# Weight conversion of the first pass: 228 interleaved items through SBUF in place of HBM-to-HBM casts and phase-wise items

## Chip, cores and metric

The kernel runs on all 8 cores of one Trainium2 chip. Each core works on its own 4096 of the 32768 tokens and on a full copy of all weights; the cores exchange nothing. The metric is the device time in microseconds of the slowest core, from one launch.

## What is computed

```python
x = x + attn(layernorm(x))          # x: [4, 8192, 2048] f32
x = x + ffn(layernorm(x))

def attn(x):                        # identity = x
    xn = (x - mu) * rsqrt(var + 1e-5) * gamma + beta
    z, gate = split(xn @ W_in.T, 2)             # W_in [8192, 2048] f32
    z = z * sigmoid(clip(z, -15, 15)) * softmax(-dt)
    return (z * silu(clip(gate, -15, 15))) @ W_out.T + x   # W_out [2048, 4096] f32

def ffn(x):                         # weights are int32 in 0..255
    deq = lambda wq, s: (wq - 128.0) * s[:, None]
    h = silu(x @ deq(wq_gate, s_gate).T) * (x @ deq(wq_up, s_up).T)   # 5632 wide
    return h @ deq(wq_down, s_down).T
```

## The kernel before

A core takes its 4096 tokens in 8 passes of 512 (NP = 8). In each pass the weights stream once from HBM in slabs of 128 x 2048 bf16, 512 KB each, 304 slabs per pass, through a ring of 7 buffers wb (NWB). SyncE issues all slab loads in the order of their use (gen_sync), each after the matmuls of the slab seven places earlier are done. A pass has these stages on PE (gen_tensor): transposes of the normalized tokens (xn4, then xnT); the in projection, 32 gate iterations e of two slabs (z and gate) with 16 matmuls each; the out projection in two halves P2 of 32 slabs for 256 tokens each; transposes again; the gate and up projections, 44 iterations h of two slabs (wg, wu); the down projection in two halves of 44 slabs (wd).

VectorE works in program order (gen_vector2): first the softmax of dt and the statistics of the first LayerNorm (ln1_block); then for each e the clipping and products of the gate (label gat:p:e); for each P2 the residual and the statistics of the second LayerNorm (st2:p:P2); for each h the product actb (actf:p:h); at the end the final sums. PE may be two iterations ahead of VectorE in both loops, since it waits for gat of e-2 and actf of h-2.

The matmuls read bf16 copies of the weights in HBM, called win_s, wout_s, wg_s, wu_s and wd_s. They are made once, during the first pass (p = 0), and every core makes them for itself. There are two ways. The float32 weights win (64 slabs) and wout (32) are cast by DMAs from HBM to HBM that GpSimd issues at the start: 16 of 4 slabs and 4 of 8 slabs. The int32 weights go through SBUF, one item per slab, 132 items. For each item GpSimd issues a load (qld) of 1024 KB into one of two buffers qi; VectorE converts it into one of two buffers qo (wq_op: subtract 128, for wd also times the scale sdbt); GpSimd stores qo to HBM and issues the load of the item two further on:

```python
            for i_ in range(3 * NH):
                u.wait(E, f"wqts:{i_}")            # conversion i_ done
                ii = E.dma_start(wq_dst(i_), qo[i_ % 2][:, :]) if E else None
                u.inc(f"qo{i_ % 2}", 16, f"wqst:{i_}", ii)
                if i_ + 2 < 3 * NH:
                    qld(i_ + 2)
```

The items come in the order all wg, all wu, all wd. VectorE's program places them: two after each gate iteration e, 12 after each P2, two after each of the first 22 iterations h. SyncE's slab loads of the first pass wait for the cast of their chunk (semaphores wc, oc), or for gdone, udone and ddone, which GpSimd raises when all 44 items of a kind have landed.

Of the kernel before, what the change touches and what calls it, by code (L numbers as in the profile page):

```python
# [63 lines left out]
def build_program():  # L64
# [27 lines left out]
    with contextlib.ExitStack() as st:  # L92
        def sb(name, shape, dt):
# [30 lines left out]
                     + [f"qo{i}" for i in range(2)]  # L124
                     + [f"x{i}" for i in range(8)]
                     + [f"wc{i}" for i in range(16)]
                     + [f"oc{i}" for i in range(4)])
# [55 lines left out]
        def gen_gpsimd(E):  # L183
# [15 lines left out]
            for c in range(16):  # L199
                i = None  # L200
                if E:
                    src = winT[4 * c:4 * c + 4].rearrange("E p c -> (E p) c")
                    dst = win_s[4 * c:4 * c + 4].rearrange("E p c -> (E p) c")
                    i = E.dma_start(dst, src, max_dma_last_dim=8192)
                u.inc(f"wc{c}", 16, f"cast:win:{c}", i)
                if c == 3:
                    u.wait(E, "dtwrow")
                    dma("dt2", dtw_s[:, :], dt_row, label="dtwst")
                    u.wait(E, "dtwst")
                    in_ap = dtw_s[:, :].rearrange("a (j p) -> p (a j)", p=128) if E else None  # L210
                    i2 = E.dma_start(dtwt[:, 0:NZ], in_ap, allow_slow_non_contiguous=True) if E else None
                    u.inc("dt3", 16, "dtwcols", i2)
            for c in range(4):
                i = None
                if E:
                    src = woutT[1024 * c:1024 * (c + 1), :]
                    dst = wout_s[1024 * c:1024 * (c + 1), :]
                    i = E.dma_start(dst, src, max_dma_last_dim=8192)
                u.inc(f"oc{c}", 16, f"cast:wout:{c}", i)

            def wq_src(i_):
                if i_ < NH:
                    return wqg[i_]
                if i_ < 2 * NH:
                    return wqu[i_ - NH]
                k = i_ - 2 * NH
                return wqd[k * 128:(k + 1) * 128, :]

            def wq_dst(i_):
                if i_ < NH:  # L230
                    return wg_s[i_]
                if i_ < 2 * NH:
                    return wu_s[i_ - NH]
                k = i_ - 2 * NH
                return wd_s[k * 128:(k + 1) * 128, :]

            def qld(i_):
                ii = E.dma_start(qi[i_ % 2][:, :], wq_src(i_)) if E else None
                u.inc(f"qi{i_ % 2}", 16, f"qld:{i_}", ii)
# [3 lines left out]
            for i_ in range(3 * NH):  # L243
                u.wait(E, f"wqts:{i_}")
                ii = E.dma_start(wq_dst(i_), qo[i_ % 2][:, :]) if E else None
                u.inc(f"qo{i_ % 2}", 16, f"wqst:{i_}", ii)
                if i_ + 2 < 3 * NH:
                    qld(i_ + 2)
                if i_ in (NH - 1, 2 * NH - 1, 3 * NH - 1):
                    u.wait(E, f"wqst:{i_ - 1}")  # L250
                    u.wait(E, f"wqst:{i_}")
                    if E:
                        E.sem_inc(sems["g"], 1)
                    u.inc("g", 1, {NH - 1: "gdone", 2 * NH - 1: "udone", 3 * NH - 1: "ddone"}[i_], None)
            u.wait(E, f"wqts:{3 * NH - 2}")
            dma("x6", xslot(1, 2), x_in[T + 256:T + 384, :], label="xin:1:2")
            u.wait(E, f"wqts:{3 * NH - 1}")
# [172 lines left out]
        def gen_vector2(E):  # L430
# [6 lines left out]
            def wq_op(i_):  # L437
# [3 lines left out]
                if i_ < 2 * NH:  # L441
# [270 lines left out]
```

How the kernel before makes its waits and increments, by code:

```python
    def inc(self, sem, n, label=None, instr=None):  # L47
# [5 lines left out]
                assert self.lab[label] == (sem, self.cnt[sem]), (label, self.lab[label], sem, self.cnt[sem])  # L53
        if instr is not None:
            instr.then_inc(self.sems[sem], n)
# [1 line left out]
    def wait(self, E, label):  # L57
        if E is None:
            return
        sem, val = self.lab[label]
        E.wait_ge(self.sems[sem], val)
# [121 lines left out]
        def gen_gpsimd(E):  # L183
# [80 lines left out]
                        u.wait(E, f"fin:{p}:{tc}" if j == 3 else f"finj:{p}:{tc}:{j}")  # L264
                        ii = E.dma_start(out_hbm[r0:r0 + 128, j * T:(j + 1) * T],
                                         gsc[2 * j + 1][:, :]) if E else None
                        u.inc(f"od{j}", 16, f"oD:{p}:{tc}:{j}", ii)
                    if p + 2 < NP:
                        r1 = (p + 2) * T + tc * 128
                        ii = E.dma_start(xslot(p + 2, tc), x_in[r1:r1 + 128, :]) if E else None
                        u.inc(f"x{4 * (p % 2) + tc}", 16, f"xin:{p + 2}:{tc}", ii)
            if E:
                for jj in range(4):
                    E.wait_ge(sems[f"od{jj}"], u.cnt[f"od{jj}"])
# [156 lines left out]
            def op(fn, label=None):  # L431
                if E:
                    E.wait_ge(sems["v"], u.cnt["v"])
                i = fn() if E else None
                u.inc("v", 1, label, i)
# [123 lines left out]
            def op(fn, label=None):  # L559
                if E:
                    E.wait_ge(sems["s"], u.cnt["s"])
                i = fn() if E else None
                u.inc("s", 1, label, i)
```

## Time and profile before

| | us |
|---|---|
| timed runs, lowest and highest of 2 | 8082.6 and 8993.11 |
| their median | 8537.86 |
| profiled execution | 8093.98 |
| its span, slowest core | 8092.3 |
| spans of the 8 cores | 8056.6 to 8092.3 |
| mean granted PE clock | 0.903 to 0.907 |
| PE busy | 6723.5 (83%) |
| VectorE busy | 1992.1 (25%) |
| ScalarE busy | 923.4 (11%) |

All cores do the same work on other tokens, and end within 0.5% of each other. The profile shows the slowest core, and splits its span: the granted clock is a share of full speed (1.0 is 2.4 GHz), the DMA share is the mean busy share of the core's 16 DMA engines. POOL is GpSimd, DVE is VectorE, ACT is ScalarE, SPq is SyncE's DMA queue; busy microseconds stand per engine, and an idle time in square brackets names what ended it.

### The profile page before, as it was taken

How to read it: one execution, taken by the hardware profiler on the slowest of the kernel's cores; microseconds unless marked ns; L12 is line 12 of the kernel's file. 1: busy time of each engine (PE TensorE's matmuls, PEld its weight loads, DVE VectorE, ACT ScalarE, POOL GpSimd, SP SyncE). 2: the span in 40 equal slices, each digit the busy share in tenths (PEclk: the TensorE clock that was granted, in tenths of full speed). 3: DMA queues.
4: the chain of work that ended last, by engine and by line, in shares of the span. 5: the costliest groups of instructions: out<-in, count | busy, mean ns of one | idle time of the engine just before them, and what ended most of it. 6: DMA issues, size and time to landing. Idle time of an engine off the chain costs nothing.

```text
span 8092.3 us, 83398 instructions; the slowest of 8 cores (8056.6 to 8092.3 us)
## 1 busy us (share of the span) xinstructions
PE 6723.5 (83%) x30208; PEld 2977.7 (37%) x30208; DVE 1992.1 (25%) x3488; ACT 923.4 (11%) x1330; POOL 246.1 (3%) x458
## 2 busy tenths in 40 slices
PE   1026646799889998999799998999799989999898
PEld 0002212344334443444344443444344434444343
DVE  1014333214311232114211331114211431123210
ACT  1000010002111111011100111011110211111100
POOL 1001111000000000000000000000000000000000
PEclk8568878899999998999899998999899999999898
DMA  9999979785636754484546654584547563665447
GB/s 149 109 179 306 304 254 306 254 258 175 213 125 197 237 186 150 154 283 151 184 152 224 212 195 143 169 267 160 178 152 265 171 208 130 202 213 184 154 152 238
DMA packets 416528, 1606.83 MB, mean 199 GB/s; under 512 B 46224, under 2 KB 46320, under 8 KB 395008
## 3 DMA queue, kind: packets, MB, share of 16 engines
q1 hardware_dynamic: 350208, 1275.22, 48.5%
q0 software_dynamic: 65920, 326.28, 16.0%
q8 instruction: 250, 4.10, 0.2%
q14 instruction: 150, 1.23, 0.1%
HBM read 1548.87 MB, written 153.11 MB: 210 GB/s over the span
## 4 chain that ended last, share of the span: by engine, by line
PE 74%; DMA 10%; DVE 6%; another core or an unknown queue 6%; issue 2%; ACT 2%; POOL 1%; DVEq 0%; ACTq 0%; POOLq 0%; SPq 0%
PE pb L315 74%; DMA qi<-wqg 3%; DMA qi<-wqd 3%; DMA qi<-wqu 3%; ACT xnT L578 1%; DVE gsc L508 1%; DVE bnb L456 1%; DMA out<-gsc 1%; DVE qo L442 1%; DVE qo L444 1%; DVE xres L511 1%; DVE gsc L553 0%; ACT xn L602 0%; ACT xnT L607 0%
## 5 line engine op out<-in xcount | busy, mean ns | idle before, releaser
L315 PE MATMUL pb<-xnT,wb 128*128 128x512 bf16 x19456 | 4341.7, 387 | 714.8 <-DVE actb L497 542.1
L315 PEld LDWEIGHTS pb<-xnT,wb 128*128 128x128 bf16 x19456 | 1930.5, 99 | 3122.4 <-issue 918.7
L315 PE MATMUL pb<-wb,actb 128*128 128x512 bf16 x9728 | 2215.6, 390 | 253.4 <-DVE gsc L553 70.7
L315 PEld LDWEIGHTS pb<-wb,actb 128*128 128x128 bf16 x9728 | 967.1, 100 | 1500.4 <-issue 449.3
L535 DVE SCALAR_TENSOR_TENSOR actb<-pb,suct,gsc 128x512 bf16<-128x512 f32 x352 | 264.2, 751 | 2165.2 <-PE pb L315 2162.7
L616 ACT ACTIVATE gsc<-pb,sgct 128x512 f32<-128x512 f32 x352 | 242.4, 689 | 2322.4 <-PE pb L315 2322.3
L315 PE MATMUL pb<-idmt,xn 128*128 128x128 bf16 x1024 | 167.5, 291 | 382.5 <-ACT xn L602 165.4
L588 ACT ACTIVATE gsc<-gsc 128x512 f32<-128x512 f32 x256 | 161.5, 631 | 1941.1 <-DVE gsc L492 1941.0
L492 DVE TENSOR_SCALAR gsc<-pb 128x512 f32<-128x512 f32 x256 | 177.0, 691 | 618.7 <-PE pb L315 558.5
L442 DVE TENSOR_SCALAR qo<-qi 128x2048 bf16<-128x2048 int32 x88 | 108.0, 1227 | 697.3 <-DMA qi<-wqg 518.5
L265 POOL DMA_DIRECT2D out<-gsc x128 | 69.0, 540 | 6463.0 <-DVE gsc L553 6442.7
L315 PEld LDWEIGHTS pb<-idmt,xn 128*128 128x128 bf16 x1024 | 80.1, 115 | 473.1 <-issue 472.1
L495 DVE TENSOR_TENSOR gsc<-gsc 128x512 f32<-128x512 f32 x256 | 177.1, 692 | 255.1 <-ACT gsc L590 255.1
L578 ACT ACTIVATE xnT<-pb,bcct,gcct 128x512 bf16<-128x512 f32 x128 | 99.8, 780 | 913.6 <-PE pb L315 901.9
L497 DVE SCALAR_TENSOR_TENSOR actb<-gsc,dtwt 128x512 bf16<-128x512 f32 x256 | 192.2, 751 | 26.9 <-DVE gsc L496 0.5
L493 DVE TENSOR_SCALAR gsc<-pb 128x512 f32<-128x512 f32 x256 | 176.8, 690 | 28.5 <-DVE gsc L492 1.9
L496 DVE TENSOR_TENSOR gsc<-pb,gsc 128x512 f32<-128x512 f32 x256 | 177.1, 692 | 26.6
L553 DVE TENSOR_TENSOR gsc<-xres,pb 128x512 f32<-128x512 f32 x64 | 44.0, 687 | 539.1 <-PE pb L315 492.0
L590 ACT ACTIVATE gsc<-gsc 128x512 f32<-128x512 f32 x256 | 161.5, 631 | 43.4 <-DVE gsc L493 42.3
L444 DVE SCALAR_TENSOR_TENSOR qo<-qi,sdbt 128x2048 bf16<-128x2048 int32 x44 | 100.8, 2292 | 175.5 <-DMA qi<-wqd 175.3
L508 DVE TENSOR_SCALAR gsc<-xres,coef 128x512 f32<-128x512 f32 x64 | 35.0, 546 | 364.9 <-PE pb L315 358.4
L553 DVE TENSOR_TENSOR gsc<-qi,pb 128x512 f32<-128x512 f32 x32 | 22.0, 687 | 342.8 <-PE pb L315 322.9
(77 smaller groups left out, 955.0 us busy)
## 6 DMA issues: line engine op xcount, KB each, us to landing
wb<-wd_s SPq DMA_DIRECT2D x704, 512.0 KB, 5.2
wb<-win_s SPq DMA_DIRECT2D x512, 512.0 KB, 3.3
wb<-wout_s SPq DMA_DIRECT2D x512, 512.0 KB, 4.8
wb<-wg_s SPq DMA_DIRECT2D x352, 512.0 KB, 3.3
wb<-wu_s SPq DMA_DIRECT2D x352, 512.0 KB, 3.3
qi<-wqg POOLq DMA_DIRECT2D x44, 1024.0 KB, 11.2
qi<-wqu POOLq DMA_DIRECT2D x44, 1024.0 KB, 10.5
qi<-wqd POOLq DMA_DIRECT2D x44, 1024.0 KB, 9.9
```

The source lines that it names most:

```text
L315: i = E.matmul(out_ap, lhsT, rhs, start=start, stop=stop) if E else None
L442: op(lambda i_=i_: E.tensor_single_scalar(qo[i_ % 2][:, :], qi[i_ % 2][:, :], -128.0, OP.add), f"wqts:{i_}")
L444: op(lambda i_=i_: E.scalar_tensor_tensor(qo[i_ % 2][:, :], qi[i_ % 2][:, :], -128.0, sdbt[:, :], OP.add, OP.mult), f"wqts:{i_}")
L492: op(lambda pz=pz, b=b: E.tensor_scalar(gsc[b][:, :], pz[:, :], 15.0, -15.0, OP.min, OP.max), f"zc:{p}:{e}")
L493: op(lambda pg=pg, b=b: E.tensor_scalar(gsc[b + 2][:, :], pg[:, :], 15.0, -15.0, OP.min, OP.max), f"gc:{p}:{e}")
L495: op(lambda b=b: E.tensor_tensor(gsc[b][:, :], gsc[b + 2][:, :], gsc[b + 3][:, :], OP.mult))
L496: op(lambda pz=pz, b=b: E.tensor_tensor(gsc[b + 2][:, :], pz[:, :], gsc[b + 1][:, :], OP.mult))
L497: op(lambda b=b, e=e: E.scalar_tensor_tensor(actb[:, e * T:(e + 1) * T], gsc[b + 2][:, :], dtwt[:, e:e + 1], gsc[b][:, :], OP.mult, OP.mul ...
L535: op(lambda h=h: E.scalar_tensor_tensor(actb[:, h * T:(h + 1) * T], pb[2 * (h % 2) + 1][:, :], suct[:, h:h + 1], gsc[4 * (h % 2)][:, :], O ...
L578: op(lambda k=k: E.activation(xnT[:, k * T:(k + 1) * T], pb[4 + k % 2][:, :], AF.Identity, scale=gcct[:, k:k + 1], bias=bcct[:, k:k + 1]), ...
L588: op(lambda b=b: E.activation(gsc[b + 1][:, :], gsc[b][:, :], AF.Sigmoid), f"sz:{p}:{e}")
L616: op(lambda h=h: E.activation(gsc[4 * (h % 2)][:, :], pb[2 * (h % 2)][:, :], AF.Silu, scale=sgct[:, h:h + 1]), f"sil:{p}:{h}")
```

## The change

All weights now go through SBUF as items of one list, ITEMS, 228 of them: for each e the two win slabs and the wout slab, then for each h the slabs of wg, wu and wd. The HBM-to-HBM casts are gone. conv_op takes the place of wq_op and has a third form, a tensor_copy from float32 to bf16 for win and wout. VectorE's program places the items: 6 after the first statistics, three after each gate iteration e up to e = 29 (those of e + 2), 18 after each P2, and three after each of the first 32 iterations h. GpSimd issues the first two loads ahead of the store of the dt weights. Its loop now waits, ahead of store i, for store i-1 to have landed, and raises the semaphore g then (label cf), so that each slab load of SyncE in the first pass waits for just its own item. Stores take four semaphores in turn (qs). Nothing else differs; the seven later passes are the same.

```diff
+        ITEMS = []
+        for e in range(NZ):
+            ITEMS.append(("win", 2 * e))
+            ITEMS.append(("win", 2 * e + 1))
+            ITEMS.append(("wout", e))
+        for h in range(NH):
+            ITEMS.append(("wg", h))
+            ITEMS.append(("wu", h))
+            ITEMS.append(("wd", h))
...
-            for c in range(16):
...
-                    i = E.dma_start(dst, src, max_dma_last_dim=8192)
...
-            for i_ in range(3 * NH):
+            for i_ in range(NIT):
+                if i_ >= 1:
+                    u.wait(E, f"wqst:{i_ - 1}")
+                    if E:
+                        E.sem_inc(sems["g"], 1)
+                    u.inc("g", 1, f"cf:{i_ - 1}", None)
                 u.wait(E, f"wqts:{i_}")
-                ii = E.dma_start(wq_dst(i_), qo[i_ % 2][:, :]) if E else None
-                u.inc(f"qo{i_ % 2}", 16, f"wqst:{i_}", ii)
-                if i_ + 2 < 3 * NH:
+                ii = E.dma_start(item_dst(i_), qo[i_ % 2][:, :]) if E else None
+                u.inc(f"qs{i_ % 4}", 16, f"wqst:{i_}", ii)
+                if i_ + 2 < NIT:
                     qld(i_ + 2)
...
                     if p == 0:
-                        if kind == "win":
-                            u.wait(E, f"cast:win:{item[1] // 4}")
...
-                        elif kind == "wu":
-                            u.wait(E, "udone")
...
+                        u.wait(E, f"cf:{item_of_slab(kind, item[1])}")
...
+                if kind in ("win", "wout"):
+                    op(lambda i_=i_: E.tensor_copy(qo[i_ % 2][:, :], qi_f32[i_ % 2]), f"wqts:{i_}")
...
                     ln1_block(0)
+                    u.wait(E, "cst")
+                    for i_ in range(6):
+                        conv_op(i_)
...
-                    if p == 0:
-                        wq_op(2 * e)
-                        wq_op(2 * e + 1)
+                    if p == 0 and e + 2 < NZ:
+                        for i_ in range(3 * (e + 2), 3 * (e + 2) + 3):
+                            conv_op(i_)
...
-                        for k in range(12):
-                            wq_op(64 + 12 * P2 + k)
+                        for k in range(18):
+                            conv_op(3 * NZ + 18 * P2 + k)
...
-                    if p == 0 and h < 22:
-                        wq_op(2 * NH + 2 * h)
-                        wq_op(2 * NH + 2 * h + 1)
+                    if p == 0 and h < 32:
+                        for i_ in range(3 * NZ + 36 + 3 * h, 3 * NZ + 36 + 3 * h + 3):
+                            conv_op(i_)
```

GpSimd at the start, after the input tokens and constants; s_v counts VectorE's instructions, s_dt2 the store of the dt weights. Before:

```order
L185 DMA actb<-dtr 1x16x256
L204 DMA win_s<-winT 512x2048 x4
L185 DMA dtw_s<-actb 16x1x256 [waits s_v]
L211 DMA dtwt<-dtw_s 128x32x1 [waits s_dt2]
L204 DMA win_s<-winT 512x2048 x12
L218 DMA wout_s<-woutT 1024x2048 x4
L238 DMA qi0<-wqg 128x2048
L238 DMA qi1<-wqg 128x2048
L245 DMA wg_s<-qo0 128x2048 [waits s_v]
L238 DMA qi0<-wqg 128x2048
L245 DMA wg_s<-qo1 128x2048 [waits s_v]
```

and now, where s_qs0 to s_qs3 count the stores:

```order
L227 DMA actb<-dtr 1x16x256
L242 DMA qi0<-winT 128x2048
L242 DMA qi1<-winT 128x2048
L227 DMA dtw_s<-actb 16x1x256 [waits s_v]
L251 DMA dtwt<-dtw_s 128x32x1 [waits s_dt2]
L260 DMA win_s<-qo0 128x2048 [waits s_v]
L242 DMA qi0<-woutT 128x2048
L260 DMA win_s<-qo1 128x2048 [waits s_qs0,s_v]
L242 DMA qi1<-winT 128x2048
L260 DMA wout_s<-qo0 128x2048 [waits s_qs1,s_v]
```

The 20 cast DMAs ahead of the first load of qi are gone, and every store after the first has a wait for the store before it.

VectorE from the end of the first statistics through the first gate iteration, before:

```order
L480 TENSOR_SCALAR coef<-ntmp 128x4 [waits s_v]
L492 TENSOR_SCALAR gsc0<-pb0 128x512 [waits s_t,s_dt3,s_v]
L493 TENSOR_SCALAR gsc2<-pb1 128x512 [waits s_v]
L495 TENSOR_TENSOR gsc0<-gsc2,gsc3 128x512 [waits s_s,s_v]
L496 TENSOR_TENSOR gsc2<-pb0,gsc1 128x512 [waits s_v]
L497 SCALAR_TENSOR_TENSOR actb<-gsc2,dtwt,gsc0 128x512 [waits s_v]
L442 TENSOR_SCALAR qo0<-qi0 128x2048 [waits s_qi0,s_v]
L442 TENSOR_SCALAR qo1<-qi1 128x2048 [waits s_qi1,s_v]
L492 TENSOR_SCALAR gsc4<-pb2 128x512 [waits s_t,s_v]
```

and now:

```order
L447 CAST qo0<-qi0 128x2048 [waits s_cst,s_qi0,s_v]
L447 CAST qo1<-qi1 128x2048 [waits s_qi1,s_v]
L447 CAST qo0<-qi0 128x2048 [waits s_qi0,s_qs0,s_v]
L447 CAST qo1<-qi1 128x2048 [waits s_qi1,s_qs1,s_v]
L447 CAST qo0<-qi0 128x2048 [waits s_qi0,s_qs2,s_v]
L447 CAST qo1<-qi1 128x2048 [waits s_qi1,s_qs3,s_v]
L502 TENSOR_SCALAR gsc0<-pb0 128x512 [waits s_t,s_dt3,s_v]
L503 TENSOR_SCALAR gsc2<-pb1 128x512 [waits s_v]
L505 TENSOR_TENSOR gsc0<-gsc2,gsc3 128x512 [waits s_s,s_v]
L506 TENSOR_TENSOR gsc2<-pb0,gsc1 128x512 [waits s_v]
L507 SCALAR_TENSOR_TENSOR actb<-gsc2,dtwt,gsc0 128x512 [waits s_v]
L447 CAST qo0<-qi0 128x2048 [waits s_qi0,s_qs0,s_v]
```

Six conversions stand ahead of the first gate, and the last row is the first of the three that follow each gate in place of two.

VectorE in the feed-forward loop, around its first iterations, before:

```order
L442 TENSOR_SCALAR qo1<-qi1 128x2048 [waits s_qi1,s_qo1,s_v]
L535 SCALAR_TENSOR_TENSOR actb<-pb1,suct,gsc0 128x512 [waits s_t,s_s,s_v]
L444 SCALAR_TENSOR_TENSOR qo0<-qi0,sdbt 128x2048 [waits s_qi0,s_qo0,s_v]
L444 SCALAR_TENSOR_TENSOR qo1<-qi1,sdbt 128x2048 [waits s_qi1,s_qo1,s_v]
L535 SCALAR_TENSOR_TENSOR actb<-pb3,suct,gsc4 128x512 [waits s_t,s_s,s_v]
L444 SCALAR_TENSOR_TENSOR qo0<-qi0,sdbt 128x2048 [waits s_qi0,s_qo0,s_v]
L444 SCALAR_TENSOR_TENSOR qo1<-qi1,sdbt 128x2048 [waits s_qi1,s_qo1,s_v]
```

and now:

```order
L451 SCALAR_TENSOR_TENSOR qo0<-qi0,sdbt 128x2048 [waits s_qi0,s_qs2,s_v]
L449 TENSOR_SCALAR qo1<-qi1 128x2048 [waits s_qi1,s_qs3,s_v]
L449 TENSOR_SCALAR qo0<-qi0 128x2048 [waits s_qi0,s_qs0,s_v]
L451 SCALAR_TENSOR_TENSOR qo1<-qi1,sdbt 128x2048 [waits s_qi1,s_qs1,s_v]
L543 SCALAR_TENSOR_TENSOR actb<-pb1,suct,gsc0 128x512 [waits s_t,s_s,s_v]
L449 TENSOR_SCALAR qo0<-qi0 128x2048 [waits s_qi0,s_qs2,s_v]
L449 TENSOR_SCALAR qo1<-qi1 128x2048 [waits s_qi1,s_qs3,s_v]
L451 SCALAR_TENSOR_TENSOR qo0<-qi0,sdbt 128x2048 [waits s_qi0,s_qs0,s_v]
L543 SCALAR_TENSOR_TENSOR actb<-pb3,suct,gsc4 128x512 [waits s_t,s_s,s_v]
```

Each product of the loop is followed by three conversions, one of each kind of weight, in place of two of wd.

## Rows read from the trace of the kernel before

**Rows 1.** Stretches: us, busy per engine (x instructions), PEclk, DMA share, GB/s.
```profile
55.00:529.00 474.00, 34.66 (x160) 15.80 (x160) 24.61 (x83) 23.40 (x23) 13.18 (x20) 0.58 0.99 120
531.00:955.00 424.00, 259.95 (x936) 102.56 (x937) 185.07 (x217) 39.12 (x62) 66.41 (x124) 0.81 0.94 301
...
1045.00:1130.00 85.00, 51.12 (x199) 19.74 (x197) 14.61 (x13) 3.93 (x2) 11.96 (x22) 0.89 0.99 327
1130.00:1158.00 28.00, 5.82 (x32) 2.26 (x32) 21.51 (x61) 6.28 (x17) 1.05 (x2) 0.50 0.22 87
1158.00:1217.00 59.00, 11.86 (x48) 4.31 (x48) 14.56 (x12) 12.20 (x20) 11.96 (x22) 0.53 0.83 282
...
1236.00:1533.00 297.00, 194.66 (x733) 78.00 (x732) 117.61 (x68) 15.84 (x23) 45.38 (x86) 0.84 0.94 306
1533.00:1672.00 139.00, 138.25 (x640) 62.49 (x640) 15.33 (x21) 13.78 (x20) 1.06 (x2) 1.00 0.51 170
...
1855.00:8092.00 6237.00, 5780.18 (x26368) 2583.63 (x26368) 1528.56 (x2854) 783.47 (x1143) 70.99 (x132) 0.94 0.57 187
```

**Rows 2.** Chain that ended last, in order of time: start, us, what.
```profile
147.07 382.31 another core or an unknown queue
```

**Rows 3.** Waits, 0 to 2500 us: total, times, longest.
```profile
PE pb L315 <- DVE actb L497: 566.7, 32, 381.7
...
PE pb L315 <- DMA wb<-wu_s: 51.8, 1, 51.8
```

**Rows 4.** Instructions in order of time, gate loop of the first pass: start, us.
```profile
537.36 0.75 DVE L497 SCALAR_TENSOR_TENSOR actb<-gsc,dtwt 128x512 bf16<-128x512 f32 x1
...
602.57 1.23 DVE L442 TENSOR_SCALAR qo<-qi 128x2048 bf16<-128x2048 int32 x1 [5.42 <-DMA qi<-wqg]
...
604.35 0.54 POOL L245 DMA_DIRECT2D wg_s<-qo  x1 [5.60 <-DVE qo L442]
...
604.88 0.53 POOL L238 DMA_DIRECT2D qi<-wqg  x1
...
608.94 8.75 PE L315 MATMUL pb<-xnT,wb 128*128 128x512 bf16 x32 [4.32 <-DVE actb L497]
...
952.52 0.75 DVE L497 SCALAR_TENSOR_TENSOR actb<-gsc,dtwt 128x512 bf16<-128x512 f32 x1
...
1016.87 0.55 DVE L508 TENSOR_SCALAR gsc<-xres,coef 128x512 f32<-128x512 f32 x1 [56.71 <-PE pb L315]
```

**Rows 5.** The same view, VectorE, twelve conversions with nothing beside them.
```profile
1157.84 2.56 DVE L442 TENSOR_SCALAR qo<-qi 128x2048 bf16<-128x2048 int32 x2
1168.67 1.23 DVE L442 TENSOR_SCALAR qo<-qi 128x2048 bf16<-128x2048 int32 x1 [8.28 <-DMA qi<-wqu]
...
1215.64 1.23 DVE L442 TENSOR_SCALAR qo<-qi 128x2048 bf16<-128x2048 int32 x1 [4.14 <-DMA qi<-wqu]
```

**Rows 6.** The same view, VectorE, feed-forward loop of the first pass.
```profile
1236.16 4.68 DVE L444 SCALAR_TENSOR_TENSOR qo<-qi,sdbt 128x2048 bf16<-128x2048 int32 x2
...
1531.95 1.62 DVE L535 SCALAR_TENSOR_TENSOR actb<-pb,suct,gsc 128x512 bf16<-128x512 f32 x2
...
1671.49 0.75 DVE L535 SCALAR_TENSOR_TENSOR actb<-pb,suct,gsc 128x512 bf16<-128x512 f32 x1 [6.16 <-PE pb L315]
```

**Rows 7.** The same view, VectorE and PE, start of the program.
```profile
83.94 0.17 DVE L480 TENSOR_SCALAR coef<-ntmp 128x4 f32<-128x4 f32 x1
...
107.67 15.61 PE L315 MATMUL pb<-xnT,wb 128*128 128x512 bf16 x64 [1.27 <-ACT xnT L578]
```

**Rows 8.** DMA issues, 531 to 955 us, then 1158 to 1217: KB each, us to landing.
```profile
wb<-win_s SPq DMA_DIRECT2D x51, 512.0 KB, 8.2
wg_s<-qo POOLq DMA_DIRECT2D x44, 512.0 KB, 7.0
...
wu_s<-qo POOLq DMA_DIRECT2D x11, 512.0 KB, 4.6
```

More of the change, by code:

```diff
@@ L123, in build_program @@
                      + [f"qi{i}" for i in range(2)]
[L124 to L127, printed above, removed]
+                     + [f"qs{i}" for i in range(4)]
+                     + [f"x{i}" for i in range(8)])
         sems = {n: st.enter_context(nc.semaphore("s_" + n)) for n in sem_names}
@@ L162, in build_program, with item_of_slab, item_src, item_dst @@
         NSLAB = len(slab_list(0))
+        ITEMS = []
[7 more added lines that the diff above has]
+            ITEMS.append(("wd", h))
+        NIT = len(ITEMS)
+        def item_of_slab(kind, idx):
+            if kind == "win":
+                return 3 * (idx // 2) + (idx % 2)
+            if kind == "wout":
+                return 3 * idx + 2
+            base = 3 * NZ
+            off = {"wg": 0, "wu": 1, "wd": 2}[kind]
+            return base + 3 * idx + off
+        def item_src(i_):
+            kind, idx = ITEMS[i_]
+            if kind == "win":
+                return winT[idx]
+            if kind == "wout":
+                return woutT[idx * 128:(idx + 1) * 128, :]
+            if kind == "wg":
+                return wqg[idx]
+            if kind == "wu":
+                return wqu[idx]
+            return wqd[idx * 128:(idx + 1) * 128, :]
+        def item_dst(i_):
+            kind, idx = ITEMS[i_]
+            if kind == "win":
+                return win_s[idx]
+            if kind == "wout":
+                return wout_s[idx * 128:(idx + 1) * 128, :]
+            if kind == "wg":
+                return wg_s[idx]
+            if kind == "wu":
+                return wu_s[idx]
+            return wd_s[idx * 128:(idx + 1) * 128, :]
         def newton_rsqrt(E, op, vp_ap, w, iters):
@@ L198, in gen_gpsimd @@
             dma("dt1", dt_row, dtr_in[:, :], label="dtin")
-            for c in range(16):
[L200 to L203, printed above, removed]
-                    i = E.dma_start(dst, src, max_dma_last_dim=8192)
[L205 to L235, printed above, removed]
             def qld(i_):
-                ii = E.dma_start(qi[i_ % 2][:, :], wq_src(i_)) if E else None
+                ii = E.dma_start(qi[i_ % 2][:, :], item_src(i_)) if E else None
                 u.inc(f"qi{i_ % 2}", 16, f"qld:{i_}", ii)
@@ L242, in gen_gpsimd @@
             qld(1)
-            for i_ in range(3 * NH):
-                u.wait(E, f"wqts:{i_}")
-                ii = E.dma_start(wq_dst(i_), qo[i_ % 2][:, :]) if E else None
-                u.inc(f"qo{i_ % 2}", 16, f"wqst:{i_}", ii)
-                if i_ + 2 < 3 * NH:
-                    qld(i_ + 2)
-                if i_ in (NH - 1, 2 * NH - 1, 3 * NH - 1):
+            u.wait(E, "dtwrow")
+            dma("dt2", dtw_s[:, :], dt_row, label="dtwst")
+            u.wait(E, "dtwst")
+            in_ap = dtw_s[:, :].rearrange("a (j p) -> p (a j)", p=128) if E else None
+            i2 = E.dma_start(dtwt[:, 0:NZ], in_ap, allow_slow_non_contiguous=True) if E else None
+            u.inc("dt3", 16, "dtwcols", i2)
+            for i_ in range(NIT):
+                if i_ >= 1:
                     u.wait(E, f"wqst:{i_ - 1}")
-                    u.wait(E, f"wqst:{i_}")
                     if E:
                         E.sem_inc(sems["g"], 1)
-                    u.inc("g", 1, {NH - 1: "gdone", 2 * NH - 1: "udone", 3 * NH - 1: "ddone"}[i_], None)
-            u.wait(E, f"wqts:{3 * NH - 2}")
+                    u.inc("g", 1, f"cf:{i_ - 1}", None)
+                u.wait(E, f"wqts:{i_}")
+                ii = E.dma_start(item_dst(i_), qo[i_ % 2][:, :]) if E else None
+                u.inc(f"qs{i_ % 4}", 16, f"wqst:{i_}", ii)
+                if i_ + 2 < NIT:
+                    qld(i_ + 2)
+            u.wait(E, f"wqst:{NIT - 1}")
+            if E:
+                E.sem_inc(sems["g"], 1)
+            u.inc("g", 1, f"cf:{NIT - 1}", None)
+            u.wait(E, f"wqts:{NIT - 2}")
             dma("x6", xslot(1, 2), x_in[T + 256:T + 384, :], label="xin:1:2")
-            u.wait(E, f"wqts:{3 * NH - 1}")
+            u.wait(E, f"wqts:{NIT - 1}")
             dma("x7", xslot(1, 3), x_in[T + 384:T + 512, :], label="xin:1:3")
@@ L435, in op, with conv_op @@
                 u.inc("v", 1, label, i)
-            def wq_op(i_):
+            def conv_op(i_):
                 u.wait(E, f"qld:{i_}")
```

11 lines of the change are left out of this document (2 added, 9 removed).

## Prediction

> **What bounds the kernel now.** I read the profile in this order: the stretches of the first pass, the chain that ended last, the waits, then the instructions in order of time. The whole story is in the first pass. In the table of stretches [rows 1] the seven later passes take 6237 us, 891 us each, with PE 5780 us busy. The first pass takes 1855 us. Look down its last three columns: from 55 to 529 us the DMA engines are 0.99 busy and PE works 35 us of 474; from 531 to 955 and from 1236 to 1533 they are 0.94 busy at 301 and 306 GB/s, PE idles over a third of the time. PE sets the pace only between 1533 and 1672 us, where DMA falls to 0.51. The chain [rows 2] says the same: it rests for 382 us on a transfer it cannot name, the casts from HBM to HBM, and then goes from one load of qi to the next. The longest wait of PE there is for actb of VectorE [rows 3], and VectorE in turn waits for the loads of qi (5.42 us before one conversion, [rows 4]): PE is held by conversions, these by DMA. So the question is not when PE starts but how many DMA-microseconds the first pass holds, and where the DMA engines rest.
>
> **The pace of one item.** An item is a load of 1024 KB and a store of 512 KB, 1.573 MB. Two paces can be read. With one gate iteration (two slabs) beside every two items: the last gate instruction runs at 537.36 us for e=0 and 952.52 us for e=31 [rows 4], 415.2/31 = 13.4 us per iteration. With nothing beside it: VectorE converts at 1168.67 and nine items later at 1215.64 [rows 5], 5.2 us per item. In the feed-forward loop 22 iterations fill 1236.16 to 1531.95 [rows 6], 13.44 us each.
>
> **What is removed.** The casts of win and wout, 48 MiB written and 96 read, between 55 and 529 us. With them goes an idle stretch of VectorE, ACT and PE. Also gone is the single release of all wu slabs after the last wu item: PE waited 51.8 us for it [rows 3], of which 19 us lay between VectorE's last conversion of the block (1215.64 + 1.23, [rows 5]) and the next (1236.16, [rows 6]).
>
> **What is added.** 96 items for the same weights. At 5.2 us that is 499 us of the DMA engines against the 474 us removed: the work is moved, not saved. Bounds for an added item: 1.573 MB at 327 GB/s, the best rate of any stretch [rows 1], is 4.8 us; half an iteration of 13.4 us is 6.7 us. I take 5.2, the pace measured by itself. The cast on VectorE has no row; its nearest ones are the int32 conversions, 1.23 us with one operand [rows 4] and 2.3 with two (4.68 for a pair, [rows 6]). Either is far under 5.2 and lies beside the next load, so its cost is nothing while DMA is the pace.
>
> **The new timeline.** First-pass statistics end on VectorE at 84.1 us [rows 7]. Six items follow; in the block that began at 1157.84 the third conversion began 10.8 us later [rows 5], and three more at 5.2 make 26.4, so 84 + 27 = 111 us. PE has its transposed input at 107.67 [rows 7] and its first two slabs, and e=0 takes about 7 us. Gate 0 takes 5 us more: the first loop conversions begin at 120 us.
> Thirty iterations carry three items and two slabs: 13.4 + 5.2 = 18.6 us, 558 us in all, to 678. The last win item must still be stored, loaded and multiplied and gate 31 made: about 15 us, 693. First half of the out projection: from the last gate (952.52 + 0.75) to 1016.87, where VectorE takes the result [rows 4], 64 us with a stall for slabs beside conversions that now lies elsewhere; 60 us, 753. Residual and statistics 28 us, the stretch 1130 to 1158 [rows 1]: 781. Then 18 items instead of 12 beside the second half: the twelve took 85 us (1045 to 1130), six more at 5.2 are 31, so 897. Statistics again, 925. 18 items alone: 59 + 31 = 90, 1015. The feed-forward loop goes on at once: 32 iterations of 13.44 + 5.2 = 18.64 are 597 us, 1612. PE is two iterations ahead then, so ten remain of 44. Twenty lay between 1531.95 + 1.62 and 1671.49 + 0.75 [rows 6], 6.93 each: 69 us, 1681. Before, that point was 1672. Net +9 us.
>
> **The new wait on GpSimd.** Store i is now issued only after store i-1 landed; behind it stand the load of item i+2 and all later ones, and VectorE waits for those. Beside slabs a store lands 7.0 us after its issue, and items come 6.7 us apart; alone it lands after 4.6 us, and items come 5.2 apart [rows 5, 8]. So the wait may push a store by up to about 0.5 us. Bounds: 0, if the DMA queue holds a load meanwhile (it does: the load was issued 0.5 us after the previous store, [rows 4]), and 0.5 x 228 = 114 us. Where DMA is 0.94 to 0.99 busy, a store issued a little later finds the engines still at work; I cost it only in the 42 items outside the two loops (6 + 18 + 18), since conversions by themselves leave DMA at 0.83 [rows 1]: 21 us. Below nothing it cannot be: it only delays.
>
> **Sum.** The profiled execution took 8093.98 us (span 8092.3). 8094 + 9 + 21 = 8124 us, I say 8120. The median of the two timed runs is 8537.86, between 8082.6 and 8993.11; the profiled execution agrees with the lower one within 0.2%, and my numbers stand beside that one. A difference under 2% (162 us) is about what a measurement of this kernel cannot tell from none.
>
> **Rivals.**
> *The stores pace the items (slower).* If a store lands 7.0 us after issue also when it is issued alone in line, the spacing is 7.0 + 0.54 for the issue = 7.6 us. An iteration of three items is then 22.8 instead of 18.6, over 62 iterations +260 us: 8380. For it: 7.0 is above today's 6.7. Against it: those 7.0 us are mostly queueing behind the 1 MB load and slabs; without slabs they are 4.6 [rows 8]. It decides from a mean spacing of 6.9 us in the loops (0.7 x 186 items = 130 us).
> *PE is late with the slab chain (no change in class).* Conversion to store 1.8 us [rows 4], store 7.0, slab 8.2 [rows 8], half a gate's matmuls 4.4 (8.75 for 32 matmuls, [rows 4]): 21.4 us, against some 25 us from the second conversion of an iteration (12 us into its 18.6) to the gate after the next. If transfers lengthen by 20% under the load, VectorE waits 3 us in half the iterations: +45, 8165.
> *The cast holds back GpSimd (no change in class, at its edge).* The 96 fp32 casts on VectorE could keep GpSimd from issuing the next load while they run: 96 x 1.23 = 118 us if none of it is hidden, 8240. Against it: the int32 conversion, at 0.6 ns per element, is as fast an operation, and a store issued right behind it takes 0.54 us, the load after it 0.53 [rows 4]. The Trainium skill (SBUF — State Buffer, section "SBUF: two separate sides") says that a two-port fp32 copy on VectorE locks GpSimd out of writing descriptors, so that the DMA engines sit idle. No row here shows such a copy; the rows beside the int32 conversion show no issue drawn out.
> *DMA never rests (faster).* The first pass moves 228 x 1.573 + 304 x 0.524 + about 14 = 532 MB. If all stretches ran at 327 GB/s from 40 us on, the pass would end at 1667 instead of 1855: 7906. For it: early interleaving gives PE work from 108 us. Against it: VectorE's statistics and the loop's closed chain leave 6% unused in both long stretches, and the ten last iterations leave half.
> No stretch of [rows 1] is above 327 GB/s. The Trainium skill (HBM Reference, section "Specifications (TRN2)") gives about 358 GB/s per core with both cores of a pair streaming. By that the same bytes would end the pass at 1526 us, an estimate of 7765; I give it 0.01, since saturated stretches at 0.99 stay at 327.
>
> **How the numbers follow.** The forecast has 0.60, the stores 0.15, the slab chain 0.10, the held-back GpSimd 0.06, DMA that never rests 0.06 (with the 0.01 above), anything else 0.03. Range: below, items at 4.8 us in loops and blocks (104 x 0.4 = 42) and 60 us for less idle DMA, 8018; above, an added item at 6.7 us in both loops (62 x 1.5 = 93) and half of the store wait's upper bound (57, less the 21 counted), 8249. I give 8015 to 8260. Faster by over 2%: 0.07; within 2%: 0.77; slower: 0.16.
>
> **What would show it.** PE busy from about 108 us on, the loop of gates ending near 693, feed-forward loop near 1681, the pass near 1865. Iterations of 18.6 us in both loops at 300 to 320 GB/s. POOL's stores should wait for VectorE, not for the store before. It is wrong if GpSimd waits mostly for its own stores with iterations over 20.5 us, if PE waits for slabs of win_s, or if DMA moves over 330 GB/s.

## The result, and the profile after

The changed kernel is 1.015 times the kernel before (95% interval 1.0105 to 1.0195). The five runs of the changed kernel behind this ratio take 8180 to 8233 us, those of the kernel before 8062 to 8094 over all rounds. That is slower by about 120 us, inside the 2% that I called no change, and outside its noise. The sum said +30.

In many runs of either kernel the PE clock of one half of the chip falls for a while and lengthens that half, so I compare, by the slowest core, only halves with a mean granted clock of 0.902 or more: the median is 8067 us over 28 halves of the kernel before and 8187 over 13 of the changed one. The profiled execution, by core (span, clock):

```profile
core 0: 8444.9 us, clock 0.874
...
core 6: 8191.0 us, clock 0.902
...
die 0 (median of its cores): 8430.5 us, clock 0.873
die 1 (median of its cores): 8183.1 us, clock 0.902
```

Core 6 is read from here on. Its stretches of the first pass, columns as in [rows 1]:

```profile
0.00:80.00 80.00, 0.00 (x0) 0.00 (x0) 32.91 (x81) 4.99 (x2) 10.59 (x22) 1.00 0.40 120
80.00:120.00 40.00, 22.82 (x111) 10.92 (x112) 11.07 (x13) 23.38 (x23) 7.16 (x12) 1.00 0.82 240
120.00:744.00 624.00, 280.69 (x960) 107.72 (x980) 219.22 (x246) 39.02 (x62) 96.83 (x180) 0.73 0.92 283
...
829.00:963.00 134.00, 50.11 (x196) 19.92 (x197) 28.41 (x18) 4.19 (x2) 18.32 (x34) 0.73 0.93 305
...
991.00:1096.00 105.00, 20.84 (x94) 8.79 (x96) 28.32 (x19) 13.00 (x21) 18.32 (x34) 0.58 0.84 274
1096.00:1722.00 626.00, 294.73 (x1004) 114.84 (x1024) 175.63 (x129) 21.99 (x32) 100.91 (x191) 0.71 0.89 294
1722.00:1796.00 74.00, 70.87 (x313) 31.70 (x320) 9.54 (x14) 6.87 (x10) 1.60 (x3) 0.96 0.50 171
```

In the first row DMA is at 0.40; in the kernel before the casts kept it at 0.89 over the same 80 us. The third is the gate loop, now with three items per iteration; it answers to the row 531 to 955 of [rows 1]. PE is still idle over half of it, and DMA is *less* busy than before, 0.92 against 0.94, at 283 GB/s against 301. The feed-forward loop, 1096 to 1722, is at 0.89 and 294 where it was at 0.94 and 306. In the last row PE sets the pace, for 74 us instead of 139.

The waits in the gate loop (total, times, longest):

```profile
PE pb L319 <- DMA wb<-win_s: 337.9, 49, 13.1
...
POOL win_s L260 <- DMA wout_s<-qo: 158.4, 30, 6.9
...
POOL win_s L260 <- DMA win_s<-qo: 104.2, 19, 6.9
POOL wout_s L260 <- DMA win_s<-qo: 98.9, 15, 8.4
...
DVE gsc L502 <- PE pb L319: 6.6, 1, 6.6
```

The three rows of POOL are 361 us and 64 waits in which GpSimd stands ahead of a store until the store before has landed. In [rows 4] it waited for the conversion. PE waits 338 us for slabs of win_s, but the last row shows that hardly anybody waits for PE: VectorE did so once, for 6.6 us. One store after the other, GpSimd in order of time:

```profile
300.91 0.54 POOL L260 DMA_DIRECT2D wout_s<-qo  x1 [5.37 <-DMA win_s<-qo]
301.44 0.55 POOL L242 DMA_DIRECT2D qi<-winT  x1
307.82 0.54 POOL L260 DMA_DIRECT2D win_s<-qo  x1 [5.84 <-DMA wout_s<-qo]
308.35 0.55 POOL L242 DMA_DIRECT2D qi<-woutT  x1
314.07 0.54 POOL L260 DMA_DIRECT2D win_s<-qo  x1 [5.16 <-DMA win_s<-qo]
```

Store, load, wait for the store, store: 6.9 and 6.3 us apart. And how long a store takes to land there:

```profile
win_s<-qo POOLq DMA_DIRECT2D x60, 512.0 KB, 6.5
...
wout_s<-qo POOLq DMA_DIRECT2D x30, 512.0 KB, 5.9
```

The median over all of them is 6.2 us. It is counted from the start of the issue, so the 0.54 us of the issue is inside it. From a landing to the start of the next store lie at least 0.67 us, and in 75 of the 89 cases of this loop at most 0.05 us more. Landing and this step make the 6.7 to 6.8 us between two items (20.1 us per iteration, a third of it): nearly every store waits for the one before.

Where the first pass went, from VectorE's instructions (means over four cores, e1 in its second run; e1 is the first experiment below). The kernel before makes its first gate at 146 us on the slowest core and then stands until 529, so its gate iterations are counted from e = 1:

| us | before | forecast | changed | e1 |
|---|---|---|---|---|
| first gate done | | 120 | 120 | 119 |
| gate iteration | 13.6 | 18.6 | 20.1 | 18.5 |
| first out-projection result | 1005 | 753 | 800 | 750 |
| first feed-forward product | 1227 | 1015 | 1095 | 1037 |
| feed-forward iteration | 13.8 | 18.6 | 19.4 | 18.8 |
| end of that loop | 1674 | 1681 | 1790 | 1713 |
| first gate of the second pass | 1870 | | 1987 | 1909 |

The 117 us of the last row are the whole difference; the later passes are as long as they were. Summed over stretches of one core each (duration times DMA share, up to that gate), the DMA engines are busy for 1678 us before, 1694 us now and 1674 in e1. Idle they are for 194, 300 and 238 us. The work was moved, not saved; the loss is idle time of the DMA engines.

### The profile page after: what moved, and what is told of

Same layout as the page of the kernel before. It is cut to its first block, busy times and chain, and to the rows that moved or that the text cites. A ratio compares the mean times of both kernels' runs of the same rounds, so it can differ in the third digit from the quotient of the medians.

```text
span 8444.9 us, 83963 instructions; the slowest of 8 cores (8174.8 to 8444.9 us)
## 1 busy us (share of the span) xinstructions
PE 6973.7 (83%) x29616; PEld 3041.7 (36%) x30208; DVE 2111.7 (25%) x3584; ACT 921.4 (11%) x1330; POOL 336.7 (4%) x630
## 3 DMA queue, kind: packets, MB, share of 16 engines
q0 software_dynamic: 80960, 426.95, 15.6%
## 4 chain that ended last, share of the span: by engine, by line
PE 72%; DMA 15%; DVE 6%; issue 3%; ACT 2%; POOL 0%; DVEq 0%; POOLq 0%; ACTq 0%; SPq 0%
PE pb L319 72%; DMA qi<-wqd 3%; DMA win_s<-qo 2%; DMA wout_s<-qo 2%; DMA qi<-woutT 2%; DMA wd_s<-qo 1%; DMA wu_s<-qo 1%; DMA wg_s<-qo 1%; ACT xnT L586 1%; DVE bnb L463 1%; DMA qi<-wqg 1%; DVE gsc L518 1%; DMA qi<-wqu 1%; DMA out<-gsc 1%; DVE qo L451 1%
## 5 line engine op out<-in xcount | busy, mean ns | idle before, releaser
L319 PE MATMUL pb<-xnT,wb 128*128 128x512 bf16 x19056 | 4463.7, 396 | 789.4 <-DVE actb L543 402.4
L319 PEld LDWEIGHTS pb<-xnT,wb 128*128 128x128 bf16 x19456 | 1961.7, 101 | 3287.8 <-issue 1391.0
L319 PE MATMUL pb<-wb,actb 128*128 128x512 bf16 x9536 | 2344.2, 408 | 233.5 <-DVE gsc L561 60.0
L319 PEld LDWEIGHTS pb<-wb,actb 128*128 128x128 bf16 x9728 | 1000.5, 103 | 1575.5 <-issue 887.9
L447 DVE CAST qo<-qi 128x2048 bf16<-128x2048 f32 x96 | 117.8, 1227 | 380.4 <-DMA qi<-winT 220.7
L449 DVE TENSOR_SCALAR qo<-qi 128x2048 bf16<-128x2048 int32 x88 | 108.0, 1227 | 371.6 <-DMA qi<-wqu 251.6
```

Source lines behind the costliest of these rows:

```text
L319: i = E.matmul(out_ap, lhsT, rhs, start=start, stop=stop) if E else None
```

## The experiments

Times are medians as above, with the number of values in brackets. The kernel before has 8067 (28); on the chips of the single rounds it has 8061 to 8071, so differences of 5 us mean nothing.

**e1: no store wait on GpSimd.** SyncE waits for the landed stores itself.

```diff
             for i_ in range(NIT):
-                if i_ >= 1:
-                    u.wait(E, f"wqst:{i_ - 1}")
-                    if E:
-                        E.sem_inc(sems["g"], 1)
-                    u.inc("g", 1, f"cf:{i_ - 1}", None)
                 u.wait(E, f"wqts:{i_}")
...
-                        u.wait(E, f"cf:{item_of_slab(kind, item[1])}")
+                        u.wait(E, f"wqst:{item_of_slab(kind, item[1])}")
```

> The changed kernel without GpSimd's wait for its last store: SyncE waits for the landed stores itself. Theory W (the wait ahead of each store holds back the store and the load behind it, about 0.5 us for each of 228 items, and so made the 122 us by which the changed kernel's first pass is longer): gate iterations fall from 20.1 to 18.6-19.0 us, feed-forward iterations from 19.6 to 18.6-18.9, the items that run alone from 5.8 to 5.0-5.3 us, and the time to 8095-8130 us, 1.00 to 1.005 of the kernel before. Rival C (the float32 items and their slab loads cost the DMA engines more than the rows of before say, the wait is hidden): all paces stay within 0.2 us and the time stays above 8175, 1.01 to 1.015 of the kernel before.

Measured: 8127 (5), 60 us under the changed kernel and 56 over the kernel before on the same chip. Core 0, the gate loop and the feed-forward loop:

```profile
120.00:693.00 573.00, 289.74 (x960) 108.45 (x980) 219.53 (x246) 39.03 (x62) 96.80 (x180) 0.77 0.99 311
1036.00:1644.00 608.00, 292.65 (x1004) 114.19 (x1024) 175.94 (x129) 21.98 (x32) 100.92 (x191) 0.73 0.91 303
```

DMA is at 0.99 and 311 GB/s in the gate loop, an iteration takes 18.6 us. That is what the forecast had for this loop, and the rival C, that float32 items cost more than they should, falls. GpSimd waits for VectorE again, and the stores come when the conversions are done; in the second run of e1, 35 of 89 stores of this loop were issued before the last one had landed (GpSimd in order of time, that run):

```profile
307.46 0.54 POOL L255 DMA_DIRECT2D win_s<-qo  x1 [7.21 <-DVE qo L438]
...
313.22 0.54 POOL L255 DMA_DIRECT2D win_s<-qo  x1 [4.68 <-DVE qo L438]
...
317.99 0.54 POOL L255 DMA_DIRECT2D wout_s<-qo  x1 [3.69 <-DVE gsc L493]
```

But 60 us is half of the loss. The feed-forward loop stays at 0.91, 18.8 us. And the items that run alone, from the third of the second block on, are 5.7 to 6.1 us apart on four cores of either run of e1 (6.1 to 6.3 in the changed kernel), not the 5.0 to 5.3 expected.

**e2: the kernel before with the wait.**

```diff
             for i_ in range(3 * NH):
+                if i_ >= 1:
+                    u.wait(E, f"wqst:{i_ - 1}")
                 u.wait(E, f"wqts:{i_}")
```

> The kernel before with one line more: GpSimd waits, ahead of store i, for store i-1 to have landed, for its 132 items. Theory W: 132 x 0.5-0.6 us = 65 to 80 us longer, 1.008 to 1.010 of the kernel before; gate iterations rise from 13.4 to 14.4-14.6 us and so do the feed-forward ones. Rival C: no change, within 20 us, iterations at 13.4.

Measured: 8095 (7), +28 us, or +24 against the kernel before on the same chip. The direction is W's, the size is not: 0.2 us per item, where I had 0.5 to 0.6, and C's limit of 20 us is missed by little. Gate iterations took 13.7 to 14.1 us, feed-forward ones 13.9 to 14.4, on three cores (13.4 to 13.8 and 13.5 to 14.1 before, on eight). The granted clock in the gate loop was 0.80, 0.71 and 0.71 on these cores, where it was 0.81 in [rows 1]; so these paces are the weaker evidence. Its waits (core 3, first 2000 us):

```profile
POOL wg_s L247 <- DMA wg_s<-qo: 180.9, 28, 8.8
...
POOL wd_s L247 <- DVE qo L446: 153.0, 23, 19.1
```

It waits for its own stores here too. But items of this kernel are 6.8 us apart anyway, which is about the pace of the stores. I read the wait as a floor under the spacing and not as a price per item: where items come 6.8 us apart it costs little, where they would come 6.2 us apart it costs the difference.

**e6: wait kept, SyncE waiting itself.** e1 changed two things; this puts the wait back alone (diff against e1).

```diff
+                if i_ >= 1:
+                    u.wait(E, f"wqst:{i_ - 1}")
                 u.wait(E, f"wqts:{i_}")
```

> The changed kernel with GpSimd's wait ahead of each store kept, but SyncE waiting for the landed stores itself, as in e1; so it differs from e1 by the wait alone and from the changed kernel by the way of the signal alone. Theory W (the wait is the cost): as the changed kernel, 8165 to 8200 us, gate iterations 19.9 to 20.3 us, feed-forward ones 19.4 to 19.7. Rival S (part of e1's gain came from slabs released without the detour over GpSimd): 8130 to 8160 us, gate iterations near 19.2.

Measured: 8158 (4), 31 us over e1 and 29 under the changed kernel, in between, but the three were measured on different chips; so I ran the changed kernel (a3), e6 and e1 again on one chip, with a fourth kernel, e7, that separates the two ways of signalling.

> The changed kernel again, beside e6, e1 and e7 on one chip, so that 35 and 40 us can be told apart. All theories: 8165 to 8200 us, gate iterations 20.0 to 20.2 us, feed-forward 19.4 to 19.6.

> e6 again (wait kept, SyncE waits for the landed stores). If its gap to the changed kernel was real: 30 to 45 us under a3, feed-forward iterations 18.8 to 19.0. If it was chance: within 15 us of a3.

> e6 with one instruction put back in GpSimd's loop: it raises the semaphore g after each landed store as in the changed kernel, but nobody waits for it. Theory Q (the extra instruction between landing and the next store lengthens each link of GpSimd's chain): as a3, 30 us or more over e6, in both loops. Rival R (slabs released later through GpSimd were what cost): as e6, within 12 us.

> e1 again (no wait, SyncE waits for the stores). Theory W: 35 to 45 us under e6_second, 70 to 85 us under a3, and 35 to 55 us over the kernel before; the gate iterations 18.5 to 18.7 us. Rival: within 20 us of e6_second.

e7 is e6 with GpSimd's signal put back, unused (diff against e6):

```diff
                 if i_ >= 1:
                     u.wait(E, f"wqst:{i_ - 1}")
+                    if E:
+                        E.sem_inc(sems["g"], 1)
+                    u.inc("g", 1)
```

Measured: changed kernel 8172 (6), e6 8179 (3), e7 8169 (5), e1 8118 (5). The single values of the first three lie between 8152 and 8199, those of e1 between 8104 and 8134. The first three are one: the gap between the changed kernel and e6 was chance or the chip, and neither Q nor R is seen. (The first gate of the second pass comes at 1969, 1955 and 1952 us, means over four cores each; a cost of R up to some 15 us stays open.) e1 stands 51 to 61 us lower, so the wait alone costs about 55 us on this chip; I had expected 35 to 45 against e6 and 70 to 85 against the changed kernel. Across chips, e6 in its first run stood 31 us over e1. The gate loop of e6 in its second run is near the changed kernel's (0.92 and 283 GB/s there):

```profile
120.00:728.00 608.00, 294.20 (x981) 109.39 (x979) 216.53 (x241) 37.77 (x60) 96.81 (x180) 0.71 0.94 288
```

**e5: the load ahead of the wait.** The diff is against e6.

```diff
-                if i_ >= 1:
-                    u.wait(E, f"wqst:{i_ - 1}")
                 u.wait(E, f"wqts:{i_}")
+                if i_ + 2 < NIT:
+                    qld(i_ + 2)
+                if i_ >= 1:
+                    u.wait(E, f"wqst:{i_ - 1}")
                 ii = E.dma_start(item_dst(i_), qo[i_ % 2][:, :]) if E else None
                 u.inc(f"qs{i_ % 4}", 16, f"wqst:{i_}", ii)
-                if i_ + 2 < NIT:
-                    qld(i_ + 2)
```

> As e6, but in GpSimd's loop the load of item i+2 is issued ahead of the wait and of store i; only the store is held by the store before. Theory L (what costs is the load held behind the waiting store): as e1, 8105 to 8135 us, gate iterations 18.5 to 18.8 us. Rival H (the held store itself costs, since the pace of stores is landing plus issue, 6.7 us, whatever the loads do): 8160 us and more, gate iterations near 20.

Measured: 8206 (2), 1.0208 times the kernel before (1.0164 to 1.0252) and 48 us over e6 on the same chip, gate iterations 20.3 to 20.9 us on the eight cores. L falls: it is not the held load that costs. But e5 changed more than the order, and that shows in GpSimd's issue of a store, by tile (count, busy us, mean ns), in the gate loop and in the feed-forward loop:

```profile
L259 POOL DMA_DIRECT2D win_s<-qo x60 | 58.6, 977 | 249.0 <-DMA wout_s<-qo 159.2 <-DMA win_s<-qo 89.8
...
L259 POOL DMA_DIRECT2D wg_s<-qo x32 | 30.7, 960 | 151.3 <-DMA wd_s<-qo 143.7 <-issue 7.5
...
L259 POOL DMA_DIRECT2D wu_s<-qo x32 | 17.2, 538 | 191.1 <-DMA wg_s<-qo 191.1
```

0.96 to 0.98 us instead of 0.54, except where the store of wu_s is issued. In order of time:

```profile
305.78 1.23 DVE L440 CAST qo<-qi 128x2048 bf16<-128x2048 f32 x1 [3.10 <-DMA win_s<-qo]
306.16 0.97 POOL L259 DMA_DIRECT2D wout_s<-qo  x1 [7.28 <-DMA win_s<-qo]
```

The store is issued while the cast runs on VectorE: both wait for the store before to land, and the load, issued early, no longer holds the cast back. Stores of wu_s are issued beside the two-operand conversion of wd (2.29 us), and take 0.54. The last section says more.

This is also where the 48 us come from, as far as the gate loop shows (means over the eight cores of e5 and of the first run of e6): stores are 6.93 us apart against 6.64, the issue takes 0.97 us against 0.54, and from the end of the issue to the landing it is 5.41 us against 5.47. The load put ahead of the store did not lengthen its landing; the drawn-out issue lengthened the chain. Without these 0.43 us the spacing would be about 6.5 us (an estimate), still nearer to e6's 6.64 than to e1's 6.20, so L falls on this count too.

**e4: early items.** e1 with 12 items ahead of the first gate.

```diff
                 for tc in range(4):
...
                     ln_stats(p, tc, 0)
+                    if p == 0 and tc in (0, 2):
+                        conv_op(tc)
+                        conv_op(tc + 1)
...
-                    for i_ in range(6):
+                    for i_ in range(4, 12):
...
-                    if p == 0 and e + 2 < NZ:
-                        for i_ in range(3 * (e + 2), 3 * (e + 2) + 3):
+                    if p == 0 and e + 4 < NZ:
+                        for i_ in range(3 * (e + 4), 3 * (e + 4) + 3):
```

> e1 with 12 items in place of 6 ahead of the first gate, four of them between the statistics, and none after the gates of e=28 to 31. Theory I (in the first pass each microsecond in which the DMA engines rest is a microsecond of the time): the engines rest some 25 to 35 us less in the first 120 us, the gate loop has six items fewer, and the time falls by 20 to 35 us against e1, to 8080 to 8105. Rival P (the start is set by the statistics and PE's first slabs, and delaying them gives the gain back): no change against e1, 8105 to 8130, with the first gate later by 10 us or more.

Measured: 8098 (4), 20 to 29 us under e1's two values. It ran on another chip than they did; against the kernel before on its own chip it is +30, where e1 is +53 and +56. The first 120 us of the kernel before, of the changed kernel (core 6) and of e4 (core 1):

```profile
0.00:120.00 120.00, 22.03 (x114) 10.92 (x115) 33.24 (x83) 25.85 (x22) 10.22 (x23) 1.00 0.93 162
```

```profile
0.00:120.00 120.00, 22.82 (x111) 10.92 (x112) 43.97 (x94) 28.37 (x25) 17.75 (x34) 1.00 0.54 160
```

```profile
0.00:120.00 120.00, 12.58 (x72) 6.75 (x73) 45.27 (x92) 25.84 (x22) 20.96 (x40) 1.00 0.67 205
```

The engines' rest falls from 55 to 40 us, less than the 25 to 35 us hoped for. The first gate comes at 140 to 146 us instead of 120, as P said, and the time falls all the same: the gate of e = 31 comes at 672 to 695 us, in e1 at 684 to 712. P falls. The time lies in theory I's range, but its microsecond for microsecond isn't shown: over the whole first pass the engines rest for 248 us in e4 and for 249 and 261 in the two runs of e1 (means over eight cores).

**d1: converted tiles straight into the slab ring.** If the first pass is paid in DMA time, slabs should not go out and come back. For win, the first half of wout, wg and wu, VectorE writes the converted tile into the wb buffer from which PE reads it, and GpSimd stores it from there; SyncE skips these 184 loads. Items are ordered by use, two per gate iteration, wd items in between.

```diff
+        DIRECT = {it[2]: n for n, it in enumerate(ITEMS) if it[2] is not None}
+        def item_tile(i_):
+            kind, idx, sl = ITEMS[i_]
+            return qo[idx % 2] if sl is None else wb[sl % NWB]
...
+                    if g in DIRECT:
+                        g += 1
+                        continue
```

> A version built on the reading that the first pass is paid in DMA-microseconds: in the first pass the converted win, wout, wg and wu tiles go straight into the ring of slab buffers, from which PE reads and GpSimd stores them, so 184 slab loads (96 MB, about 300 us at 322 GB/s) fall away; only wd items still go out and come back. Theory D (DMA time of the first pass sets it): gate iterations about 10.4 us, feed-forward iterations about 15.6 us, the first gate of the second pass near 1585 us instead of 1870, and the time 7770 to 7850 us, 0.96 to 0.97 of the kernel before. Rival E (with DMA relieved PE at its lower clock, or VectorE's program order, sets the pace): gate iterations above 14 us and a time above 7950.

Measured: 7872 (4), from 7838 to 7944; one whole run took 7891, against 8062 and 8068 of the kernel before beside it, 0.978. It beats both kernels, by less than expected. Core 3, the gate loop and the feed-forward loop:

```profile
118.00:460.00 342.00, 237.81 (x968) 98.18 (x966) 185.27 (x218) 39.04 (x62) 68.24 (x124) 0.90 0.86 284
...
778.00:1368.00 590.00, 331.86 (x1152) 128.66 (x1152) 197.92 (x145) 24.73 (x36) 114.16 (x216) 0.75 0.85 288
```

Over this core's first pass the DMA engines are busy for 1361 us, 317 less than in the kernel before, as theory D has it. But they rest for 275 us; the pass ends at 1636 to 1686 us where 1585 was expected. Gate iterations take 10.9 to 11.4 us where 10.4 was expected, feed-forward ones 16.4 to 17.8 where 15.6 was, and the DMA share is 0.86. In the gate loop the rows of one qi buffer account for this: its load lands 8.1 us after the issue (median), then come the conversion (1.23), the issue of the store (0.54) and gaps of about 0.9 us in all, and then the next load into the same buffer: 10.7 us for two items. That more qi buffers would fill the engines is not tested. E's threshold of 14 us was not reached.

## Why the prediction was right and wrong

**Right: the first pass is paid in DMA time, and the casts' share comes back as items.** 1678 us busy before and 1694 now. The gate loop without the wait is at 18.5 and 18.6 us where the working had 18.6, the first out-projection result at 750 where it had 753. The first gate came at 120 as said. Part of the 18.6 is luck. The row at 537.36 is the gate of e = 1 and not of e = 0, which was made at 146.32 before VectorE stood still:

```profile
146.32 0.75 DVE L497 SCALAR_TENSOR_TENSOR actb<-gsc,dtwt 128x512 bf16<-128x512 f32 x1
529.55 1.23 DVE L442 TENSOR_SCALAR qo<-qi 128x2048 bf16<-128x2048 int32 x1 [382.48 <-DMA qi<-wqg]
```

So the 415.2 us are 30 iterations of 13.8 us on this core (13.6 over all eight), and the added item costs 4.9 to 5.0 us in the loop and not 5.2. One error made up for most of the other.

**Wrong: the step on the new wait.** "Where DMA is 0.94 to 0.99 busy, a store issued a little later finds the engines still at work; I cost it only in the 42 items outside the two loops." The runs say the reverse. It costs about 55 us (21 were given), and most lies inside the loops: 1.1 to 1.6 us for each of 31 gate iterations, 0.3 to 0.6 for the feed-forward ones. The wait doesn't find the engines at work: the DMA share of the gate loop is 0.92 to 0.94 with it and 0.97 to 0.99 without. I compared a store's landing (7.0) with the items' old spacing (6.7), found them alike and called the wait hidden. The change, however, makes the spacing shorter, to 18.6/3 = 6.2 us, and it is with this that the spacing of the store chain, 6.7 us, had to be compared: (6.7 - 6.2) x 93 = 47 us for the gate loop. The rival "the stores pace the items" had the right mechanism and an overdrawn price. It took its landing of 7.0 us from the loop of the kernel before, and with the wait stores land after 6.2. Its 0.54 us for the issue are already inside the 7.0; what has to be added is the 0.67 us from the landing to the next store. Its mean spacing was to be 7.6 and was 6.7; the mark of 6.9 from which it was to decide was not reached. Of the signs of being wrong, GpSimd did wait mostly for its own stores, at 20.1 and not 20.5 us per iteration, and PE did wait for slabs of win_s, which by itself cost nothing.

**Mis-sized: the removed release of the wu slabs.** I booked 19 us between two conversions as saved. The stretch was not idle:

```profile
1217.00:1236.00 19.00, 7.02 (x22) 2.72 (x23) 0.70 (x1) 0.00 (x0) 1.05 (x2) 0.55 0.93 313
```

DMA was 0.93 busy in it, with the slabs that had been held back (DMA issues of that stretch):

```profile
wb<-wu_s SPq DMA_DIRECT2D x4, 512.0 KB, 9.0
wb<-wg_s SPq DMA_DIRECT2D x4, 512.0 KB, 8.3
```

Eight loads, some 13 us at 313 GB/s (an estimate). The changed kernel makes such loads too, earlier, beside the 18 items of each block: 11 of them in e1 between 775 and 1038 us. The blocks took longer than forecast, and the first feed-forward product in e1 came at 1037 instead of 1015. That the loads are the whole reason is not shown: the items of the second block were 5.7 to 6.1 us apart, against 5.2 in [rows 5], and the four slab loads beside them (6.7 us at 313 GB/s) explain a little over half of that. The feed-forward iterations at 18.8 instead of 18.64 and the last ten at 73 instead of 69 us are another 9.

**Priced inside the timeline but not seen: the start.** The engines rest 48 of the first 80 us. The sum had this in "84 + 27 = 111", and the timeline was right; but I named no price. In the first 120 us they rest for 52 us in e1 and for 9 in the kernel before, and these 43 us are most of the 53 to 66 by which e1's first pass has more rest than that of the kernel before (means over eight cores). e4 ended 20 to 29 us earlier with a busier start.

**The sum.** Forecast +30; against it the wait 34 more than given, blocks and release 22, the feed-forward loop and its tail 9, makes about +95. Measured are +107 against the kernel before on the chip of the last round and +120 in the first; the rest I can't assign to a cause, and two chips or samples differ by 15. The range, 8015 to 8260, held the time, and "no change within 2%" held too; the step and the size did not.

**Rivals.** The slab chain: PE waits 338 us for win_s slabs, but VectorE waits for PE once, 6.6 us; it costs next to nothing. The cast that holds back GpSimd: in the changed kernel an issue takes 0.54 or 0.55 us, as before, since stores and loads are issued after the conversion and not beside it; no cost there. In e5 it came true, 0.43 us per store in the gate loop. DMA that never rests: no stretch comes over 327 GB/s, and e1 reaches 0.99 only in the gate loop.

## What to carry to other kernels

A wait that looks hidden at today's spacing has to be compared with the spacing that the change itself brings: a chain of issue, landing and next issue is a floor under the pace, cheap above it (0.2 us per item in e2) and paid in full below it. Where a stage is bound by DMA, book the busy microseconds of the DMA engines on both sides, then look for new rests; an idle wait of PE or VectorE is no gain unless the DMA engines rest in it too. The gain, 2% in d1, lay in the round trip: let the first reader take the converted tile from the buffer from which it is stored. And when instructions are reordered, look at what now runs at the same moment: e5 put the issue of the stores beside the conversions.

## What the runs showed of the hardware

GpSimd's issue of a store takes 0.54 us when VectorE does nothing or runs the two-operand conversion (128x2048, 2.29 us), and 0.96 to 0.98 us on average when it is issued beside the one-operand cast or conversion (1.23 us); in the row at 306.16 it ends 0.12 us after the cast does. The Trainium skill (SBUF — State Buffer, section "SBUF: two separate sides") says that VectorE locks GpSimd out of the shared port pair while it runs a two-port operation, so that it can't write descriptors, and names the fp32 copy as one. The trace agrees with that rule for the cast, and shows the same for the one-operand int32 to bf16 form. The price here is what is left of the conversion: 0.43 us per store in e5's gate loop, and nothing in the changed kernel, where the issue comes after it (0.54 or 0.55 us).

A store of 512 KB lands 6.2 us after the start of its issue in the median of the changed kernel's gate loop, where slabs and loads run beside it, and after 3.0 us at the least. About half of the 6.7 us between two stores is thus time that a store alone doesn't need (an estimate). The landing isn't a constant of the kernel either: it was 7.0 us in the gate loop of the kernel before, where 28 of 61 stores were issued before the last one had landed, and 6.0 to 6.5 in e2 (three cores), where none was.
